# A bias added by VectorE after the row scaling instead of by TensorE to the projected features, and a negation moved from VectorE to GpSimd

## The reference

```python
# layer 1: spectral filter, adj plays the eigenvectors
x_spec = einsum('nk,nc->kc', adj, x)
x = _layernorm(x + einsum('nk,kc->nc', adj, exp(-evals * t)[:, None] * x_spec))
# layer 2: graph convolution
adj_hat = adj + eye(N)
deg = sum(adj_hat, axis=1, keepdims=True)
x = _layernorm(x + tanh((adj_hat / deg) @ (x @ W) + b))
```

## Time and profile before

| what | value |
| --- | --- |
| timed runs | 674.04, 676.32, 681.46 us; median 676.32 |
| the profiled execution's own time | 667.65 us |
| its span, first to last instruction | 665.9 us |
| busy: TensorE matmul, VectorE, ScalarE, GpSimd | 619.1, 510.2, 400.9, 360.7 us |
| mean granted TensorE clock | 0.974 of full |

### The profile page before, as it was taken

How to read it: one execution, slowest core, us unless ns; L and a number is a source line. 1 busy time by engine, 2 the same in 40 slices (tenths; PEclk the granted TensorE clock), 3 DMA queues, 4 the chain that set the end, 5 groups by cost and what they waited for, 6 DMA issues and landing times.

```text
span 665.9 us, 8247 instructions
## 1 busy us (share of the span) xinstructions
PE 619.1 (93%) x2578; PEld 469.7 (71%) x2578; DVE 510.2 (77%) x588; ACT 400.9 (60%) x883; POOL 360.7 (54%) x190
## 2 busy tenths in 40 slices
PE   3999999999984899999999999999999979999992
PEld 2888778877763575768878788788788756666661
DVE  3899888989878996868959687296486475999991
ACT  5999899999877345455535555254445335455662
POOL 0000000000325886868969889388586678896871
PEclk9999999999995999999979999799999999999997
DMA  8999999999999999799918999077987099999201
GB/s 288 387 387 386 387 387 387 387 387 387 379 299 283 292 267 299 173 282 274 265 55 230 249 285 274 4 208 204 222 212 198 23 315 326 286 328 344 84 17 47
DMA packets 141290, 174.69 MB, mean 262 GB/s; under 512 B 6852, under 2 KB 105412, under 8 KB 141256
## 3 DMA queue, kind: packets, MB, share of 16 engines
q1 hardware_dynamic: 88976, 121.68, 57.9%
q10 hardware_dynamic: 52280, 52.58, 29.3%
HBM read 172.13 MB, written 2.11 MB: 262 GB/s over the span
## 4 chain that ended last, share of the span: by engine, by line
PE 68%; DMA 8%; DVE 7%; ACT 6%; POOL 5%; issue 3%; SPq 1%; ACTq 1%; POOLq 0%; DVEq 0%
PE ps L743 13%; PE ps L745 13%; PE ps L744 13%; DMA raw<-in_adj_dram 8%; PE ps L739 8%; PE ps L719 4%; ACT hi L435 4%; PE ps L720 4%; PE ps L721 4%; POOL lo L402 3%; DVE vt L590 3%; PE ps L810 2%; PE ps L809 2%; PE ps L815 2%; PE ps L812 1%
## 5 line engine op out<-in xcount | busy, mean ns | idle before, releaser
L402 POOL TENSOR_TENSOR lo<-vt,hi 128x1024 fp32r<-128x1024 f32 x129 | 325.9, 2549 | 97.3 <-ACT hi L450 96.4
L590 DVE STREAM_TRANSPOSE vt<-raw 128x1024 f32<-128x1024 f32 x184 | 223.1, 1230 | 102.1 <-PE ps L745 79.3
L450 ACT ACTIVATE hi<-vt 128x1024 fp32r<-128x1024 f32 x163 | 169.9, 1061 | 120.6 <-DVE vt L590 99.9
L573 DVE TENSOR_TENSOR lo<-raw,hi 128x1024 fp32r<-128x1024 f32 x124 | 153.4, 1240 | 22.5 <-ACT hi L435 21.5
L435 ACT ACTIVATE hi<-raw 128x512 fp32r<-128x512 f32 x256 | 158.4, 622 | 14.8 <-DMA raw<-in_adj_dram 6.0
L719 PE MATMUL ps<-hi,xg_hi 128*128 128x512 f32 x256 | 102.6, 401 | 9.1 <-DVE lo L573 7.8
L385 POOL TENSOR_TENSOR lo<-raw,hi 128x1024 fp32r<-128x1024 f32 x4 | 10.7, 2684 | 181.5 <-ACT hi L435 181.5
L743 PE MATMUL ps<-hi,s_hi 128*128 128x512 f32 x232 | 99.2, 427 | 10.2 <-POOL lo L402 9.7
L720 PE MATMUL ps<-lo,xg_hi 128*128 128x512 f32 x256 | 100.7, 394 | 0.0
L721 PE MATMUL ps<-hi,xg_lo 128*128 128x512 f32 x256 | 100.6, 393 | 0.0
L743 PE MATMUL ps<-hi,p_hi 128*128 128x512 f32 x206 | 88.9, 432 | 6.5 <-POOL lo L402 6.4
(11 more groups left out here) (67 smaller groups left out, 558.0 us busy)
## 6 DMA issues: line engine op xcount, KB each, us to landing
raw<-in_adj_dram SPq DMA_DIRECT2D x64, 1024.0 KB, 14.2
raw<-in_adj_dram SPq DMA_DIRECT2D x88, 512.0 KB, 9.1
raw<-in_adj_dram ACTq DMA_DIRECT2D x88, 512.0 KB, 10.6
late_raw<-in_adj_dram SPq DMA_DIRECT2D x8, 512.0 KB, 11.9
late_raw<-in_adj_dram ACTq DMA_DIRECT2D x8, 512.0 KB, 13.4
xn<-in_x_dram SPq DMA_DIRECT2D x8, 256.0 KB, 12.2
x_sb<-in_x_dram SPq DMA_DIRECT2D x8, 256.0 KB, 11.8
out_dram<-x_sb ACTq DMA_DIRECT2D x8, 256.0 KB, 2.8
```

Source lines behind the costliest of these rows:

```text
L402: nc.gpsimd.tensor_tensor(lo[:, slot(p), :], vt[:, slot(p), :], hi[:, slot(p), :].bitcast(f32), ALU.subtract).then_inc(pool_lo_ready, 1)
L450: nc.scalar.activation(hi[:, slot(s), :], vt[:, slot(s), :], ACT.Copy).then_inc(hi_ready, 1)
L573: nc.vector.tensor_tensor(lo[:, q % RING1, :], raw[:, k, 2 * h:2 * h + 2, :].rearrange("p r n -> p (r n)"), hi[:, q % RING1, :].bitcast(f3 ...
L590: nc.vector.transpose(vt[:, slot(s), :].rearrange("p (m a i) -> p m a i", m=2, a=RB), load_buffer(st.load).rearrange("p (a m e i) -> p e m ...
```

## The change

The bias no longer enters `p`: the eight groups of L810 and L815 matmuls go, and with them the row of ones. In stage 3, VectorE makes `acc * rdeg + b` from the transposed sum, four `scalar_tensor_tensor` of 128 columns per ending (since 2), and signals `pre3`; ScalarE's tanh then is one activation of 512 columns with no scale. `neg_mean` is no longer made by VectorE (L657) but by GpSimd, as zero minus mean, behind `veps`; VectorE signals straight behind the four aggregations. TensorE's waits for `b` and for the ones go away, VectorE gets one for `b` at the start of the step list.

```diff
@@ gpsimd
+            nc.gpsimd.memset(zero[:, :], 0.0).then_inc(zero_ready, 1)
+            pool.wait_ge(zero_ready, 1)
-            nc.gpsimd.memset(ones[:, :], 1.0).then_inc(ones_ready, 1)
@@ inverse_deviation
                 nc.gpsimd.tensor_tensor(veps[:, par, :], mv[:, par, :, 1], eps_sb[:, :], ALU.add).then_inc(ve_sem, 1)
-                pool.wait_ge(ve_sem, n + 1)
+                nc.gpsimd.tensor_tensor(neg_mean[:, par, :], zero[:, :], mv[:, par, :, 0], ALU.subtract).then_inc(ve_sem, 1)
+                pool.wait_ge(ve_sem, 2 * n + 2)
@@ scalar, ending3
                 if since == 3:
-                    act.wait_ge(sumT_done, row + 1)
-                    act.wait_ge(deg_in, 16 * NG)
-                    for r in range(R):
-                        last = nc.scalar.activation(acc[:, r * C:(r + 1) * C], acc[:, r * C:(r + 1) * C], ACT.Tanh,
-                                                    scale=rdeg[:, g, r:r + 1])
-                    last.then_inc(tanh_ready, 1)
+                    act.wait_ge(pre3, row + 1)
+                    nc.scalar.activation(acc, acc, ACT.Tanh).then_inc(tanh_ready, 1)
@@ vector, mean_and_var
-                last.then_inc(ag_sem, 1)
-                dve.wait_ge(ag_sem, n + 1)
-                nc.vector.tensor_scalar(neg_mean[:, par, :], mv[:, par, :, 0], -1.0, None, ALU.mult).then_inc(mv_sem, 1)
+                last.then_inc(mv_sem, 1)
@@ vector, ending3
+                if since == 2:
+                    dve.wait_ge(sumT_done, row + 1)
+                    dve.wait_ge(deg_in, 16 * NG)
+                    for r in range(R):
+                        last = nc.vector.scalar_tensor_tensor(
+                            out=acc[:, r * C:(r + 1) * C], in0=acc[:, r * C:(r + 1) * C],
+                            scalar=rdeg[:, g, r:r + 1], in1=b_bc[:, :], op0=ALU.mult, op1=ALU.add)
+                    last.then_inc(pre3, 1)
@@ tensor, ending2
-                        out_t = acc2(g)[:, m * C:(m + 1) * C]
-                        nc.tensor.matmul(out_t, stage[:, 1, m * P:(m + 1) * P], w_sb[:, :], start=True, stop=False)
-                        nc.tensor.matmul(out_t, ones[:, :], b_bc[:1, :], start=False, stop=True)
+                        nc.tensor.matmul(acc2(g)[:, m * C:(m + 1) * C], stage[:, 1, m * P:(m + 1) * P], w_sb[:, :],
+                                         start=True, stop=True)
                     nc.tensor.matmul(acc3(g, g), w_sb[:, :], stage[:, 1, :].rearrange("c (m q i) -> c q m i", m=JB, q=QN),
-                                     start=g == 0, stop=False)
-                    for m in range(JB):
-                        last = nc.tensor.matmul(acc3(g, g)[:, m * P:(m + 1) * P], b_bc[:1, :], ones[:, :],
-                                                start=False, stop=g == 0 and m == JB - 1)
-                    last.then_inc(xw_done, 1)
+                                     start=g == 0, stop=g == 0).then_inc(xw_done, 1)
```

More of the change, by code:

```diff
@@ L231, in spectral_then_graph_conv @@
         saves = sb("saves", [P, 2, CW])
-        ones = sb("ones", [1, P])
         ident = sb("ident", [P, P])
@@ L246, in spectral_then_graph_conv @@
         mhalf = sb("mhalf", [P, R])
+        zero = sb("zero", [P, R])
         veps = sb("veps", [P, 2, R])
@@ L271, in spectral_then_graph_conv @@
         stored = sem("stored")
-        ident0, ident_ready, mhalf_ready, eps_ready, ones_ready = map(
-            sem, ("ident0", "ident_ready", "mhalf_ready", "eps_ready", "ones_ready"))
+        ident0, ident_ready, mhalf_ready, eps_ready, zero_ready = map(
+            sem, ("ident0", "ident_ready", "mhalf_ready", "eps_ready", "zero_ready"))
         negt_ready, ev_turned, evT_done, coef_ready = map(sem, ("negt_ready", "ev_turned", "evT_done", "coef_ready"))
@@ L279, in spectral_then_graph_conv @@
             sem, ("vturned", "hi_ready", "lo_ready", "pool_lo_ready", "mm_done"))
-        acc_out, accT_done, h_ready, st2, mv2, ag2, ve2, pw2, rs2, x1_ready = map(
-            sem, ("acc_out", "accT_done", "h_ready", "st2", "mv2", "ag2", "ve2", "pw2", "rs2", "x1_ready"))
+        acc_out, accT_done, h_ready, st2, mv2, ve2, pw2, rs2, x1_ready = map(
+            sem, ("acc_out", "accT_done", "h_ready", "st2", "mv2", "ve2", "pw2", "rs2", "x1_ready"))
         x1T_done, x1T_ready, xw_done, phi_ready, p_ready, saved = map(
             sem, ("x1T_done", "x1T_ready", "xw_done", "phi_ready", "p_ready", "saved"))
-        deg_s, sum3, sumT_done, tanh_ready, y_ready = map(
-            sem, ("deg_s", "sum3", "sumT_done", "tanh_ready", "y_ready"))
-        st3, mv3, ag3, ve3, pw3, rs3, out_ready = map(sem, ("st3", "mv3", "ag3", "ve3", "pw3", "rs3", "out_ready"))
+        deg_s, sum3, sumT_done, pre3, tanh_ready, y_ready = map(
+            sem, ("deg_s", "sum3", "sumT_done", "pre3", "tanh_ready", "y_ready"))
+        st3, mv3, ve3, pw3, rs3, out_ready = map(sem, ("st3", "mv3", "ve3", "pw3", "rs3", "out_ready"))
         def wait_lo1(eng, q):
@@ L649, in row_stats, with mean_and_var @@
                 last.then_inc(st_sem, 1)
-            def mean_and_var(par, n, st_sem, ag_sem, mv_sem):
+            def mean_and_var(par, n, st_sem, mv_sem):
                 dve.wait_ge(st_sem, n + 1)
@@ L668, in ending2 @@
                 if since == 4:
-                    mean_and_var(par, g, st2, ag2, mv2)
+                    mean_and_var(par, g, st2, mv2)
                 if since == 12:
@@ L684, in ending3 @@
                     row_stats(acc, par, st3)
-                    mean_and_var(par, row, st3, ag3, mv3)
+                    mean_and_var(par, row, st3, mv3)
+            dve.wait_ge(b_in, 16)
             for p in range(AHEAD, POSITIONS):
```

2 lines of the change are left out of this document (removed).

## The result

| | before | after |
| --- | --- | --- |
| median of the runs, us | 675.18 (666.05 to 681.46, 4 runs) | 631.62 (630.77 to 632.25, 4 runs) |
| the profiled execution's own time | 667.65 | 631.55 |
| its span; mean granted clock | 665.9; 0.974 | 628.4; 0.986 |

The ratio is 0.943, 95% interval 0.933 to 0.952: the changed kernel is faster by 5.7%. The time lies 13 us under the predicted 645, and 5 us under the low end of the range. The ratio leaves out runs that were over 1.5% above the fastest of their kernel, which occurred only in kernels that have one-row matmuls between the projections; the medians hold them.

The account below looks back on a forecast made before the run. TensorE was taken to bound stage 2 almost without a gap. 667.65 - 22.2 - 6.6 + 0.5 + 0.8 + 0.8 - 0.4 = 640.6 us, plus 4.3 for the timed runs: 645 us, range 637 to 657.

Parts of the forecast that it names:

- eight endings: TensorE's list without the bias matmuls: 2.77 us less at each ending, 22.2 us in all.
- two falls of the clock: Slow stretches at the endings of groups 2 and 4 no longer occur: 2 x 3.3 = 6.6 us gained.
- GpSimd's idle time too short: Behind endings, GpSimd's idle time may not cover what the ending becomes shorter: 0.5 us of loss booked.
- GpSimd's negations, VectorE and ScalarE in stage 3: Negations at three places where TensorE waits, +0.8 us; new VectorE instructions delaying work around rows 2 and 3, +0.8 us.
- last ending: Final chain: tanh in one saves 0.52 us, VectorE's negation goes, GpSimd's comes; sum -0.4 us.
- I keep the pace of what stays.: TensorE's endings: matmuls beside the removed records keep their pace, so 2.77 us an ending is gained.
- nothing gives more but the clock: Upper end of the endings' term: only the clock could give more than 22.2 us.
- I take half: Timed runs' median lies 8.7 us over the profiled execution (the offset); half, 4.3 us, is taken to stay.
- The rival in which the clock falls as before: Falls at the endings remain, as the page's rule suggests: 654.1 us, chance 0.18.
- GpSimd as the bound: Rival: GpSimd gives nothing back after the first four endings and its 16 negations all count: 663 us, chance 0.12.
- The new instructions held up: Rival: GpSimd's work holds up VectorE's 32 new stage 3 instructions by 2.1 us each: 704 to 708 us, chance 0.03.
- The ring: Ring of 6 steps tying other engines to TensorE; if it covers stage 3's VectorE delays, they cost 0.

Follow-up runs that it names:

- Experiments 1: Kernel before, its bias matmuls given all 128 rows of operand, zero-padded, same number and places: 647.01 us, ratio 0.962.
- 2: Kernel before, one 512-column bias matmul ahead of the projections in place of four between them, one-row L815 kept: 651.65 us, ratio 0.968.
- experiment 3: Changed kernel with four one-row matmuls adding zero put back between the projections of each ending: 658.50 us (650.03 to 661.5), ratio 0.971.
- 4: Changed kernel with four one-row matmuls adding zero put behind the projections of each ending: 642.41 us, ratio 0.955.
- number 5: The changed kernel run again, unedited: 630.80 us, ratio 0.938.
- 9: The changed kernel run a third time, unedited: 631.11 us, ratio 0.943.
- number 10: Changed kernel with ScalarE's issues of the late loads spread, one per position in place of all in a row: 631.95 us (628.37 to 633.80), ratio 0.943.
- number 6: Changed kernel with the negation back on VectorE, so only the bias has moved: 634.05 us, ratio 0.943.
- number 8: Changed kernel with all four quarters of the late buffers' first loads issued by SyncE, none by ScalarE: 633.93 us, ratio 0.943.

## Why the prediction was right and wrong

The direction and the place were right: TensorE's list bounds stage 2, what leaves an ending counts in full, and the clock no longer falls there. The size was not, since a part of the mechanism was missing. The pieces, us:

| term | predicted | found |
| --- | --- | --- |
| eight endings | -22.2 | -29.6 |
| two falls of the clock | -6.6 | -6.3 |
| GpSimd's idle time too short (all else up to the eighth ending) | +0.5 | -0.4 |
| GpSimd's negations, VectorE and ScalarE in stage 3 | +0.8, +0.8 | +0.7 together |
| last ending | -0.4 | -0.65 |
| start of stage 2, time around the span | none | -1.3, +1.4 |
| the profiled execution | 640.6 | 631.55 |
| from there to the median | +4.3 | +0.1 |

**The step that failed most: "I keep the pace of what stays."** I counted the removed records at their own length and took for granted that the projections beside them would keep 0.21 us each. They went to 0.11 and the projections' group from four stretches of 0.42 to one of 0.89 us in all: 8 x (3.70 - 2.77) = 7.4 us. The statement "nothing gives more but the clock" was wrong with it. Experiments 1 to 4 show that the cost is in the change between one-row and 128-row operands and not in the number of matmuls: with full rows between the projections their pace is restored, with zeros of one row put back it is lost, and behind them it is not.

**The second: "I take half" of the offset.** All of it went. In the 35 timed runs of before that stand beside the ten experiments, the span follows the mean clock, from 663.9 us at 0.976 to 680.1 at 0.952. A mean clock that is lower by 0.01 over some 670 us means 2 x 0.01 x 670 = 13.4 us more at half speed, of which half is lost, 6.7 us; a straight line through the 35 runs gives 5.3 us. The changed kernel's four runs lie within 1.5 us. So the offset went with time at the lower clock, as one half of my reasoning had it, and stage 1 held no part that stayed. That it was falls at the endings is likely and not shown: no trace of a slower run is kept. With both steps right the forecast would have been 640.6 - 7.4 = 633.2, 1.6 us over the result.

**The clock.** Forecast: none at 0.50 from 230 us to the products' end. Found in the profiled execution, and at every ending of stage 2 in its two repeats, which have one short stretch of 0.50 elsewhere (experiments 5 and 9). Groups 2 and 4 gave 6.84 and 6.87 us each, 3.15 beyond the 3.70. The rival in which the clock falls as before is refuted. Its page, the Trainium skill, "TensorE: Matmul & The Clock Gate", Part 1, ties a fall to idle time of the engine. No run here shows a gap in TensorE's records before the falls at the endings, and experiments 1, 2 and 4 do away with those falls and the spread. What takes them away is shown (fewer changes between the two kinds in a row); why the chip lowers the clock there is not. The ends of matmul records are modelled, and with alternating rows the same sixteen bias records and projections take 5.36 us that take 3.45 with full rows. So TensorE may stand still inside these records, and a rule of idle time is not excluded by them. A fall behind a visible wait is in the traces too, in the kernel of experiment 3 (TensorE's order, then its stretch):

```profile
526.84 0.50 PE L753 MATMUL ps<-hi,p_hi 128*128 128x512 f32 x1 [2.64 <-POOL lo L409]
```

```profile
527.00:530.80 3.80, 3.80 (x10) 0.55 1.09 347
```

There TensorE had waited 2.64 us for GpSimd, and the clock fell soon after it went on; with that one, and with those of experiments 5 and 9, the rule agrees. The wait of 2.58 us in the changed kernel's first trace brought none.

**GpSimd as the bound.** Refuted as a price, near as a fact. It sits busy without a gap through the early groups now (its order of time; the idle 3.69 and 2.47 us of the earlier trace rows are gone):

```profile
298.29 16.55 POOL L404 TENSOR_TENSOR lo<-vt,hi 128x1024 fp32r<-128x1024 f32 x6 [0.91 <-ACT hi L452]
314.79 1.19 POOL L393 TENSOR_TENSOR veps<-mv,eps_sb 128x4 f32<-128x4 f32 x1
315.93 0.20 POOL L394 TENSOR_TENSOR neg_mean<-zero,mv 128x4 f32<-128x4 f32 x1
...
317.44 31.42 POOL L404 TENSOR_TENSOR lo<-vt,hi 128x1024 fp32r<-128x1024 f32 x12
...
351.47 34.77 POOL L404 TENSOR_TENSOR lo<-vt,hi 128x1024 fp32r<-128x1024 f32 x13
```

The remainders come 0.05 to 3 us ahead of TensorE in steps 60 to 92, where it was 2 to 9, and once, behind the ending of group 3, TensorE waits some 0.4 us. The idle pieces that the prediction counted on were nearly all there, and are used up.

**The new instructions held up.** Refuted. They keep to 320 to 360 ns beside a busy GpSimd (duration min/median/max):

```profile
L679 DVE SCALAR_TENSOR_TENSOR ps<-ps,rdeg,b_bc x32: 320/350/360, 541.8 to 618.7; 128x128 f32<-128x128 f32 x32
```

The price from `L628` (344) was right. The Trainium skill, "SBUF — State Buffer", "Who interferes with whom", lets a VectorE instruction with at most one input in SBUF, outside its 2-port modes, run free of GpSimd; the row agrees, and the scalar column does not count as a second one. The prediction left that condition out. One input in SBUF is not enough by itself: the negation L657 has no more and takes up to 1.92 us; no run here shows in which mode it ran.

**Stage 3.** Booked were +0.8 and +0.8 us; TensorE lost 0.7 there against before. It now waits for a remainder of GpSimd at steps 150 and 182, where the remainder had been ready, which cost some 0.25 and 0.5 us. The ring covers the rest. On GpSimd the negation adds some 0.16 us between `veps` and `rstd` (575.91 and 576.34, against 613.17 and 613.44), not the 0.28 that was booked.

**The last ending** went as written: the new instructions are done before tanh can start, which is now one of 0.58 us in place of 1.12.

```profile
617.93 1.14 DVE L679 SCALAR_TENSOR_TENSOR ps<-ps,rdeg,b_bc 128x128 f32<-128x128 f32 x4 [5.03 <-PE ps L823]
619.11 0.58 ACT L528 ACTIVATE ps<-ps 128x512 f32<-128x512 f32 x1 [0.62 <-DVE ps L679]
```

Only that tanh now waits for VectorE, 0.62 us, and not for ScalarE's normalisation.

## What to carry to other kernels

When an instruction is taken out of a dense list, ask what it does to the pace of its neighbours as well as how long it is: the stretch from start to start with and without such a neighbour is the price, not the record's own length, and another place of the trace may show it. On TensorE put matmuls with one row of operand together, or pad the operand to full rows with zeros: here the padding alone gave 28 of the 43.6 us. And where timed runs differ by more than a kernel's own steps explain, set each run's time beside its mean clock before dividing the difference.

## What the runs showed of the hardware

- A change between a 128-row and a one-row fp32 matmul costs about 0.2 us: a projection and its bias matmul take 0.83 us when they alternate (465.65 to 466.48 in the trace of before) and 0.44 with full rows (449.13 to 449.57), so 0.39 for two changes; the table of experiments 1 to 4 holds with that price.
- Where they alternate, the granted clock can stand at 0.50 for up to about 6.6 us with no gap in TensorE's records, at endings that differ between executions (groups 2 and 4, then 5 and 6); the two falls of before cost 3.15 us each. Kernels with the alternation spread by 11 us or more between runs, those without by 1.0 to 2.4, but for number 10 with 5.4.
- A wait of TensorE of 2.4 to 2.6 us for GpSimd was followed by some 3 us at 0.50 in experiments 3, 5 and 9, and by none in the changed kernel's first trace.
- A VectorE operation of 4 columns with its operand in SBUF took 1.69 us (549.27), up to 1.92, beside GpSimd, and 0.17 at the median; the same negation on GpSimd takes 0.20.
- An issue of a transfer takes ScalarE 0.51 us at the median and up to 3.73 (number 10). Two in a row took 3.82 us (number 5) and 5.28 (number 6), eight in a row on SyncE 16.32 (number 8), long enough to starve the engines behind `hi`.
